# Two-block transformer with expert layers on one core: some token tiles sent through all experts, a channel mix woven into the attention before it, and results added by the transfers

## The reference

```python
x = x + linear_attention(norm(x))     # 16 heads, 32 features each
x = x + channel_mix(norm(x))          # sigmoid(xr @ Wr.T) * (relu(xk @ Wk.T)**2 @ Wv.T)
x = x + experts(norm(x), top=2)       # softmax gate, 8 experts, gelu, weights renormed
x = x + channel_mix(norm(x))
x = x + softmax_attention_block(norm(x))
x = x + experts(norm(x), top=1)       # silu
x = x + linear_memory(norm(x))        # decaying state, per sequence
x = x + experts(norm(x), top=1)       # the same weights again
```

## Time and profile before

| | us |
|---|---|
| three runs, median (lowest to highest) | 1011.19 (1007.5 to 1014.38) |
| the profiled execution, its own time | 1014.22 |
| its span in the profile | 1012.4 |
| linear attention ends, first mix starts | 98.6 |
| top2 from, to | 128.9, 290.0 |
| second mix from, to | 290.0, 317.5 |
| softmax attention block to | 772.7 |
| top1a to | 867 |
| linear memory to | 911.1 |
| top1b and the store of the output to | 1012.4 |

### The profile page before, as it was taken

One profiled execution on the slowest core, in us unless ns is written; L12 is line 12 of the kernel. 1 busy time (PEld: TensorE's weight loads), 2 busy tenths in 40 slices (PEclk: granted clock), 3 DMA queues, 4 the chain that ended last, 5 costly groups with the idle time before them and its releaser, 6 DMA issues.

```text
span 1012.4 us, 15306 instructions
## 1 busy us (share of the span) xinstructions
PE 815.9 (81%) x5603; PEld 492.5 (49%) x5603; DVE 687.5 (68%) x1324; ACT 530.4 (52%) x1139; POOL 183.0 (18%) x177
## 2 busy tenths in 40 slices
PE   4889835899989778888888888887797699895893
PEld 2578624499956432111111212111366499585693
DVE  6844783266577999999999888896244455656462
ACT  1530442055515847888878777787655155114252
POOL 2000027345500040000000000000030635103452
PEclk9999867899999989999999999998999699996897
DMA  4730001311120000000000000000050121100213
GB/s 115 213 108 1 0 11 47 106 54 36 38 83 1 1 1 1 1 1 1 1 1 2 1 1 1 2 1 1 1 167 1 45 81 36 44 1 22 88 36 101
DMA packets 54139, 36.73 MB, mean 36 GB/s; under 512 B 9186, under 2 KB 49314, under 8 KB 54066
## 3 DMA queue, kind: packets, MB, share of 16 engines
q1 hardware_dynamic: 49298, 25.98, 9.3%
q0 software_dynamic: 4768, 9.77, 2.9%
HBM read 22.31 MB, written 13.43 MB: 35 GB/s over the span
## 4 chain that ended last, share of the span: by engine, by line
PE 42%; issue 25%; DVE 11%; ACT 10%; POOL 6%; DMA 3%; SPq 2%; DVEq 0%; POOLq 0%; ACTq 0%
PE psum L1523 13%; PE psum L1511 9%; ACT arena L1672 7%; POOL results L1004 6%; PE psum L248 3%; PE psum L1085 3%; DVE arena L1463 2%; PE psum L1440 2%; PE psum L1095 2%; PE psum L359 2%; PE psum L337 2%; PE psum L394 1%; SPq L860 1%; PE psum L241 1%; DMA arena<-results 1%
## 5 line engine op out<-in xcount | busy, mean ns | idle before, releaser
L1463 DVE TENSOR_REDUCE arena<-psum 128x2 f32<-128x1024 f32 x256 | 298.3, 1218 | 22.1 <-PE psum L1440 21.2
L1672 ACT ACTIVATE arena<-psum 128x512 f32<-128x512 f32 x512 | 264.6, 604 | 77.3 <-PE psum L1511 77.3
L1511 PE MATMUL psum<-arena 32*128 32x512 f16 x512 | 117.8, 388 | 65.0 <-ACT arena L1672 63.6
L1128 ACT ACTIVATE arena<-psum,arena 128x128 f32<-128x128 f32 x340 | 97.0, 368 | 119.4 <-PE psum L1095 62.8
L1523 PE MATMUL psum<-arena 128*32 128x512 f32 x1024 | 138.8, 615 | 0.1
L1511 PEld LDWEIGHTS psum<-arena 32*128 32x128 f16 x512 | 29.5, 91 | 224.4 <-ACT arena L1672 201.2
L248 PE MATMUL psum<-la_wqkv,ident 128*128 128x384 f32 x316 | 116.4, 518 | 9.2 <-issue 6.7
L1440 PE MATMUL psum<-arena 32*128 32x512 f16 x512 | 108.6, 382 | 7.1 <-ACT arena L1783 4.5
L1004 POOL DMA_INDIRECT results<-arena x85 | 84.2, 991 | 110.0 <-DVE arena L1287 105.3
L996 POOL DMA_INDIRECT slots<-xn,arena x64 | 66.2, 1034 | 206.2 <-DVE arena L1205 187.6
L1085 PE MATMUL psum<-arena 128*128 128x128 f32 x680 | 95.4, 284 | 0.7 <-DVE arena L1282 0.6
(11 more groups left out here) (272 smaller groups left out, 1017.4 us busy)
## 6 DMA issues: line engine op xcount, KB each, us to landing
arena<-slots SPq DMA_DIRECT2D x19, 256.0 KB, 3.1
arena<-results SPq DMA_DIRECT2D x16, 256.0 KB, 4.2
slots<-blank SPq DMA_DIRECT2D x1, 2560.0 KB, 11.5
expert_w<-in_L_attn_b_w_dram SPq DMA_DIRECT2D x1, 2048.0 KB, 8.3
expert_w<-in_L_attn_b_w_dram SPq DMA_DIRECT2D x8, 256.0 KB, 5.1
expert_w<-in_L_ffn_W_dram SPq DMA_DIRECT2D x1, 2048.0 KB, 8.3
expert_w<-in_L_ffn_W_dram SPq DMA_DIRECT2D x8, 256.0 KB, 5.3
results<-arena POOLq DMA_INDIRECT x85
```

What stands on the lines that cost most here:

```text
L1128: last = nc.scalar.activation(self.hT[:, p, c, :], ps[:, 2 + p, c * P:(c + 1) * P], self.func, bias=own[:, FF + c:FF + c + 1])
L1463: v.tensor_reduce(self.mx[:, h % 2, keys, qt, 2 * pair:2 * pair + 2], core.psum[:, 2 * slot:2 * slot + 2, :], AX.X, ALU.max).then_inc(self ...
L1511: nc.tensor.matmul(core.psum[:, 4 + tile % self.SCORE_BANKS, :], self.kT[rows, g, at:at + P], self.qT2[rows, h % 2, :], start=True, stop=T ...
L1672: nc.scalar.activation(self.prob[:, k % self.PROBS, j, :], core.psum[:, 4 + tile % self.SCORE_BANKS, :], ACT.Exp).then_inc(self.prob_in, 1)
```

## The change

Five things are changed. First, `layer_norms` leaves half of each batch's tiles to ACT: DVE scales four (`scale_first`), ACT the other four (`scale_second`), in linear attention, both mixes and linear memory. Second, the first mix is woven into the end of linear attention, as the rows below show. Third, in top2 the first three token tiles are not sorted (`dense=3`): their 384 tokens go through all eight experts, with 384 columns per up product, and DVE adds each expert's output times the gate weight (zero for experts not chosen) to x. Then 26 indirect DMAs, 26 products in the inverse and 33 sorted tiles remain, 2 idle matmuls instead of 22 stand ahead of the loop, and MemoryWeights moves to top1a. Fourth, top1b does so with two token tiles (`dense=2`): 14 indirect DMAs, 21 sorted tiles, 7 idle matmuls instead of 11. Fifth, in top1b x (with biases and dense outputs) is stored to `results`, the indirect DMAs add their rows onto it, and the output is a copy from `results` in DRAM. Both dense blocks get 3 and 4 idle matmuls ahead of the ranks. In short:

```diff
+def scale_first(core, src, out, b, done):
+    for t in range(b * TB, b * TB + TB // 2):
+        last = core.nc.vector.tensor_scalar(out[:, t, :], src[:, t, :], ln[:, 0, t:t + 1], ln[:, 4, t:t + 1],
...
+def scale_second(core, src, out, b):
+    for t in range(b * TB + TB // 2, (b + 1) * TB):
+        last = core.nc.scalar.activation(out[:, t, :], src[:, t, :], ACT.Identity, scale=ln[:, 4, t:t + 1],
...
         self.vector_add(dve, 0)
-        self.vector_outputs(dve, 1)
+        spread(core, core.x, 0)
+        self.vector_outputs(dve, 1, range(2))
+        inverse_root(core, 4, 0)
+        offset(core, 0)
+        scale_first(core, core.x, core.xn, 0, self.behind.normed)
+        self.vector_outputs(dve, 1, range(2, 4))
+        self.behind.mix(dve, 0)
         self.vector_add(dve, 1)
...
+    SORTED_AFTER = 4
...
+        if self.dense:
+            core.claim(pe, self.xdT)
+            keep_busy(core, w, pe, self.xdT.bank, 3)
+            pe.wait_ge(self.dense_in, 1)
+            transpose_tiles(core, pe, self.xdT, [core.xn[:, t, :] for t in range(self.dense)], w.ident[:, :])
+            core.claim(pe, self.ranks)
+            keep_busy(core, w, pe, self.ranks.bank, 4)
...
+        for e in range(NE + 1):
+            if self.dense:
+                self.dense_step(pe, e)
+            if e == self.SORTED_AFTER:
+                self.invert(pe)
...
-        keep_busy(core, w, pe, 0, 11 * self.top)
+        keep_busy(core, w, pe, 0, self.idle)
...
+    def dense_step(self, pe, e):
+        if e < NE:
+            for c, turn in enumerate(self.wide[e]):
+                core.claim(pe, turn)
+                nc.tensor.matmul(ps[:, turn.bank, 0:n], self.ew.all[:, at:at + P], self.xd, start=True,
+                                 stop=True).then_inc(core.filled[turn.bank], 1)
+        if e > 0:
+            for up in self.wide[e - 1]:
+                core.moved(pe, up)
+            for t in range(self.dense):
+                for c in range(FC):
+                    last = nc.tensor.matmul(ps[:, turn.bank, t * D:(t + 1) * D],
...
+            if q == 1 and self.out is not None:
+                sp.wait_ge(self.base_in, 1)
+                sp.dma_start(self.results[0:N, :].rearrange("(t p) d -> p t d", p=P), self.core.x[:, :, :]).then_inc(self.base_out, 16)
...
+    def add_results(self, pool):
+        pool.wait_ge(self.base_out, 16)
+        for t in range(self.tiles):
+            pool.indirect_dma_start(out=target[:, :],
+                                    in_=self.y[:, t, :], in_offset=None, compute_op=ALU.add
+                                    ).then_inc(self.w.result_out[t % LANES], 16)
...
+                  Experts(core, w, w.e0, "top2", 2, ACT.Gelu_apprx_tanh, dense=3, idle=2), ChannelMix(core, w, "cm2", (27, 3), meanwhile=ValueBias(core, w)),
+                  SoftmaxAttention(core, w), Experts(core, w, w.e1, "top1a", 1, ACT.Silu, meanwhile=mw),
+                  LinearMemory(core, w, mw), Experts(core, w, w.e1, "top1b", 1, ACT.Silu, out=out, dense=2, idle=7)]
...
+            sp.dma_start(out.rearrange("b n d -> (b n) d"), w.results[0:N, :]).then_inc(stored, 16)
```

More of the change, by code:

```diff
@@ new lines, in values @@
+    def values(self, pe, b):
+        core, w = self.core, self.w
+        for g, turn in enumerate(self.t[b]["v"]):
+            core.claim(pe, turn)
+            pe.wait_ge(self.act_in, 2 * b + g + 1)
+            for i in range(4):
+                at = b * S + (4 * g + i) * P
+                last = core.nc.tensor.matmul(core.psum[:, turn.bank, i * D:(i + 1) * D], self.kact[:, at:at + P],
+                                             w.cm_wvT[:, :], start=True, stop=True)
+            last.then_inc(core.filled[turn.bank], 1)
@@ L983, in sync, with sync_last @@
         for g in range(4):
+            first = max(4 * g, self.dense)
             for k in range(self.top):
-                sp.dma_start(self.yg[:, k, 4 * g:4 * g + 4, :], rows[:, k, 4 * g:4 * g + 4, :]
+                sp.dma_start(self.yg[:, k, first:4 * g + 4, :], rows[:, k, first:4 * g + 4, :]
                              ).then_inc(self.w.back[g], 16)
+    def sync_last(self, sp):
+        for s in range(self.tiles - LANES, self.tiles):
+            sp.wait_ge(self.w.result_out[s % LANES], self.result_count(s))
     def gpsimd(self, pool):
@@ L993, in gpsimd @@
         for k in range(self.top):
-            for t in range(T):
+            for t in range(self.dense, T):
                 at = k * T + t
@@ L1097, in tensor, with invert @@
                 last.then_inc(core.filled[4 + p], 1)
+    def invert(self, pe):
+        core = self.core
+        core.claim(pe, self.inverse)
+        pe.wait_ge(self.in_tile, 3)
+        choices = [k * T + t for k in range(self.top) for t in range(self.dense, T)]
+        part = self.top * 4
+        for n, i in enumerate(choices):
+            if n == 0 or i // part > choices[n - 1] // part:
+                pe.wait_ge(self.in_row, i // part + 1)
+            last = core.nc.tensor.matmul(core.psum[:, self.inverse.bank, 0:3 * self.tiles], self.row_hot[:, i, :],
+                                         self.tile_hot[:, i, :, :], start=(n == 0), stop=(n == len(choices) - 1))
+        last.then_inc(core.filled[self.inverse.bank], 1)
@@ new lines, in scalar_dense @@
+    def scalar_dense(self, act):
+        core, n = self.core, self.dense * P
+        for e in range(NE):
+            if e >= 2:
+                core.result(act, self.narrowed[e - 2])
+            for c, turn in enumerate(self.wide[e]):
+                at = e * EW + FF + c
+                core.result(act, turn)
+                core.nc.scalar.activation(self.hd[:, e % 2, c, :], core.psum[:, turn.bank, 0:n], self.func,
+                                          bias=self.ew.all[:, at:at + 1]).then_inc(core.emptied[turn.bank], 1)
@@ new lines, in add_dense @@
+    def add_dense(self, dve, e):
+        core, turn = self.core, self.narrowed[e]
+        if e == 0:
+            dve.wait_ge(self.normed, 1)
+            dve.wait_ge(self.turned, 1)
+        else:
+            core.moved(dve, self.narrowed[e - 1])
+        core.vsync()
+        core.result(dve, turn)
+        for t in range(self.dense):
+            last = core.nc.vector.scalar_tensor_tensor(out=core.x[:, t, :], in0=core.psum[:, turn.bank, t * D:(t + 1) * D],
+                                                       scalar=self.wh[:, t, e:e + 1], in1=core.x[:, t, :],
+                                                       op0=ALU.mult, op1=ALU.add)
+            if t < self.dense - 1:
+                core.vmark(last)
+        last.then_inc(core.emptied[turn.bank], 1)
@@ L1257, in vector @@
         v.tensor_tensor(self.place_int, choice, own, ALU.add).then_inc(self.places_in, 1)
+        if self.dense:
+            for e in range(self.SORTED_AFTER, NE):
+                self.add_dense(dve, e)
         if self.meanwhile:
@@ L1266, in vector @@
                             ALU.add).then_inc(core.emptied[turn.bank], 1)
+        if self.out is not None:
+            for turn in self.bias:
+                core.moved(dve, turn)
+            dve.engine_nop().then_inc(self.base_in, 1)
         dve.wait_ge(self.ew.weights_in, self.ew.weights_all)
@@ L1291, in vector @@
                 take_weights(t)
+        if self.out is not None:
+            return
         for turn in self.bias:
```

384 lines of the change are left out of this document (264 added, 120 removed).

## The result

The changed kernel takes 1036.36 us (median of four runs, 1033.71 to 1041.82), the kernel before 1010.66 beside it: a ratio of 1.026, 95% interval 1.020 to 1.032. It is 26 us slower. I had forecast 992, in a range of 977 to 1008. The profiled execution took 1041.82 us, with a span of 1039.3.

A forecast was written before the change was run, and what follows sets the result against it. Bound taken: mostly PE's stream (42% of the chain), with waits ahead of the loops. Terms -0.3 - 10.0 - 18.0 - 1.9 + 6 - 0.9 + 10.9 - 4.9 = -19.1 from 1014.2: 995.1, as median 992; range 977 to 1008.

The forecast's parts named there:

- woven mix: End of linear attention and first mix: batch 0's statistics fill DVE's waits; -10.0 us, bounds -7 to -11.
- MemoryWeights in top1a: Top1a, between inverse and turn: its chain moves the loop start from 810.1 to near 816; +6 us, bounds +3 to +10.
- tail: End of top1b: adding transfers, then a copy within DRAM; -4.9 us, bounds -6 to +2.
- So PE is done near 178.4 ... the loop starts near 183.0: Top2 ahead of its loop: eight dense steps of 5.3 us and the inverse; loop start 183.0 instead of 198.08.
- PE idle in dense steps for semaphores: A sign that the forecast is wrong: in dense steps PE idles for ACT, DVE or semaphores; no size given.
- Top1b: Ahead of top1b's loop dense work does not fit: start near 963.2, not 948.9, +14.3 us; the block's sum +10.9.
- (1): Late hand-overs in top2's dense steps, like DVE's 14.2 us remote wait: gain falls by 8 to 14 us; chance 0.13.
- (2): Adding transfers slower than 1.93 us per tile: at 2.4 each the last loop is 10 us longer; chance 0.12.
- (3): Dense phases of top2 and top1b at 1.2 GHz: their 71.4 us double, 1035 at 60%; chance 0.08.
- (4): Top1b's dense work fits in the waits and MemoryWeights is hidden: 14.3 and 6 fall to about 4 together; chance 0.14.
- (5): The woven mix only moves DVE's waits: -2 us instead of -10, total 1000; chance 0.08.
- the dense additions: Top2, DVE's adds beside the scatters: if each of eight groups delays one by 1 us, scatters end near 179; sum unchanged.

The follow-up runs named there:

- paused: The change without dense tiles in top1b, POOL pausing about 4 us (12 small memsets) after every eighth indirect DMA of top2; 996.57 us.
- paused3: The kernel of paused (change without dense tiles in top1b, pauses in top2) timed again; 987.29 us, 0.983 of the kernel before.
- paused_all: The whole change with a pause after the eighth indirect DMA of every dense block; 1000.6 us against 1004.7, 0.996 of the kernel before.
- scatter_late: The change, but top2's 26 indirect DMAs wait until DVE has added the last dense output; 1051.99 us.
- every13: As short_pause, but one 1.5 us pause after the thirteenth indirect DMA of top2 instead of one after every eighth; 1009.99 us.
- short_pause: As paused3 with 5 memsets (about 1.5 us) instead of 12 in each pause; 988.3 us.
- before_paused: The kernel before with a 1.5 us pause after every eighth of its 32 indirect DMAs in top2; ratio 0.999.
- no_dense2: The change with dense=3 in top2 undone alone (39 tiles, 32 indirect DMAs, 22 idle matmuls); 1021.94 us against 1009.37.
- one_each: The change without dense tiles in top1b, one 128x128 memset after each indirect DMA of top2; 986.98 us, later 987.66 in rounds (0.983).

## Why the prediction was wrong

**Right by its own steps.** The woven mix (-10.7 with the scalings, -10.3 forecast), the second mix (-1.9) and linear memory (-0.9), the two loops (-11.0 and -4.8), MemoryWeights in top1a (+4.4 for +6, the ranges hold). The tail's -3.4 lies near -4.9; the missing part is POOL, behind by its 1.65 us per adding transfer. Top2's reload gave nothing instead of 1.3.

**The step that failed.** "So PE is done near 178.4 ... the loop starts near 183.0." The sum of durations was right: with the indirect DMAs out of the way, PE ended when I said (idle matmuls from 181.06). What was wrong is that the durations hold beside them. PE reached the idle matmuls at 203.1 and the first up product came at 206.6, 23.6 us late against my 183.0 (the table counts from the block's start and has 23.4). PE idle in dense steps for semaphores was among the signs that I had named for being wrong. The cause had a row in my groups, the 14.2 us of L1265, and was my first rival: priced at 8 to 14 us in all, because I took the lateness as one of single hand-overs. It is a jam: once some 32 records are outstanding PE goes on at one record per 0.7 to 2.1 us, for 20 us. The slow PE then fell to 1.2 GHz, which is part of the 22 us: the inverse took 7.82 us in the change and 5.95 in `paused`. I had held against this rival that top1a shows nothing of it:

```profile
798.47 0.96 POOL L996 DMA_INDIRECT slots<-xn,arena  x1 [0.30 <-issue]
799.11 2.48 DVE L1265 TENSOR_TENSOR x<-x,psum 128x512 f32<-128x512 f32 x4 [1.69 <-PE psum L1064]
```

That is so: beside the tenth DMA of that block the bias additions begin as soon as their products are over (799.0). But it is one place, and behind it PE had only 11 idle matmuls, 22 records, whose completions nobody waits for and which are too few to fill up. Since the hold-up comes in one execution and not in the next of the same kernel (`paused`, `paused3`), one clean place was weak evidence.

**Top1b, a wrong size as well.** +14.3 was forecast, +32.0 came. 11.1 of the difference are the hold-up (paused_all). The remaining 6.6, read from the timeline of `paused_all`: ranks end 1 us later than I had, since the three idle matmuls ran at 1.2 GHz (3.88 us); dense steps and inverse 4.1 more, with 2.26 for ACT, which was still writing `xn` and loading its tables, and two steps at the low clock; the idle matmuls wait 1.4 more for a bank that DVE's bias additions empty and run 1.7 longer. These make 8.2; the forecast's own 1.3 for the first transposes was 0.8 too much, and it counted the start before from 37.8, where the table has 38.7. My own sum had already said that this block loses 10 us; it should have told me that this part of the change is bad whatever else happens.

**The rivals.** (1) was the right mechanism, at a chance of 0.13 and at 8 to 14 us where it cost 33. (2), slow adding transfers, is real but worth 2 to 3 us, not 10: the loop is itself 1.9 us per tile. (3), dense phases at 1.2 GHz: the clock was at the low level in the stalls (from 155 to 179 us), as their effect, since PE had slowed at 153.3; it was 1.00 in scatter_late. (4), room in top1b, did not happen, with pauses neither. (5) too: the mix did what it says. And the dense additions did not hold the indirect DMAs up by 1 us each, as the prediction weighed: the longest of the 26 in top2 after the first took 1.30 us, the others 0.96 to 1.26.

## What to carry to other kernels

A stretch in which an engine waits is not free room for work until the same work has been seen to run beside what it waits for. Where a profile shows waits that no engine's work explains ("remote"), find what runs beside them before more work is put there. Here the work fitted once POOL left 0.2 us more between its indirect DMAs, which costs less than it gives back; and dense tiles pay only where the wait is about as long as their products, in top2 (0.983 of the time before with them and the memsets, 0.992 with none at all, about 10 us, though not timed beside each other) and not in top1b. And where one profile shows a hold-up gone, look at a second: here the same kernel had it in one and not in the other.

## What the runs showed of the hardware

TensorE's completions (its semaphore updates, as the trace has them) can be held back while GpSimd issues indirect DMAs of 128 rows 1.27 us apart. In both dense blocks of the change the first late one was due beside the seventh DMA in a row (over at 144.7, acted on at 147.69; over at 939.8, acted on at 941.35). After some 32 further records TensorE itself comes down to one record per 0.7 to 2.1 us. In these blocks, in the kernel before and in `paused` all was free again 1.3 to 3.5 us after GpSimd had done with the last DMA ahead of a pause or of the block's end; in `every13` a pause of 1.5 us was not enough. It appeared in top2 of the kernel before, in both dense blocks of the change, in top1b of `scatter_late`, in `every13`, and, for 3 and 4 us, in `paused`. It did not appear in the profiles with the DMAs 1.47 or 2.0 us apart, in `short_pause`, `paused3`, `paused_all` and `before_paused` with a pause after every eighth, or with plain DMAs of the same size from GpSimd or SyncE. The DMA engines had no backlog: each DMA's rows moved 0.6 us after GpSimd had finished with it, the 26th like the first, and their share was 0.14 in the whole stretch.

Such DMAs do not always do it. In `no_dense2` completions were late by 2 to 3 us, and then 44 records of idle matmuls went through at full pace beside eleven more DMAs 1.27 us apart. The kernel of `paused` and `paused3` had the lateness in one profile and not in the other.

What in the chip fills up was not found. The runs leave open whether the distance or the length of an unbroken run decides: `one_each` lowers the rate, `short_pause` shortens the run, and neither had it. Every memset here also makes GpSimd wait for a semaphore of its own before it goes on; a wait without a memset was not tried, so the time between the DMAs and that wait are not told apart. Every run here comes with the profiler's span and clock, so whether its own records of TensorE's instructions take part was not tried either.
